# Routed layers of a six-stage Trainium2 kernel: rooms for experts' results, order of the tail, second chunk's norm and the next stage's accumulating loads

## The reference, cut to what matters

```
x = x + 0.5 * routed(norm(x))      # stage routed0
x = x + attention0(norm(x))        # stage attention0, one head, causal, rank 32
x = x + 0.5 * routed(norm(x))      # stage routed1, same weights
x = x + 0.5 * gated(norm(x))       # stage gated0, inner width 704
x = x + attention1(norm(x))        # 16 heads of 128, causal, rotary
x = x + 0.5 * gated(norm(x))       # stage gated1
norm(x)   = (x - mean) / sqrt(var + eps)
routed(x) = sum over each row's 4 chosen of 16 experts (at most 128 rows each):
              w * (silu(x Wg) * (x Wu)) Wd          # inner width 176
            + (silu(x Sg) * (x Su)) Sd              # shared, inner width 352
```

## Time and profile before

| | us |
|---|---|
| median of 3 runs (lowest, highest) | 2019.42 (2014.98, 2020.13) |
| the profiled execution, its own time | 2020.47 |
| its span in the profile | 2018.7 |
| PE busy | 1938.0 (96%) |
| DVE, ACT, POOL busy | 1435.0, 1316.5, 936.9 |

### The profile page before, as it was taken

The page is one execution under the profiler, slowest core; times in us unless marked ns, Lnnn a source line. Parts: engine busy times, 40 slices in busy tenths (PEclk is TensorE's granted clock), DMA queues, the critical chain, the costliest instruction groups (busy, mean ns, idle before and its releaser), DMA issues.

```text
span 2018.7 us, 40238 instructions
## 1 busy us (share of the span) xinstructions
PE 1938.0 (96%) x13726; PEld 1763.0 (87%) x13726; DVE 1435.0 (71%) x3587; ACT 1316.5 (65%) x3367; POOL 936.9 (46%) x961
## 2 busy tenths in 40 slices
PE   7988989898999999999999999999999999999999
PEld 5768867787899999999999999999999999998888
DVE  8368763755878777787877778787777878777753
ACT  4336633444778777777877777787777778776752
POOL 2641126444454536555453645545364554536242
PEclk9999989999999999999999999999999999999999
DMA  7750068500000000000000000000000000000000
GB/s 267 219 100 1 33 195 209 144 1 9 9 9 6 10 6 4 7 9 9 6 9 7 4 7 9 9 7 9 7 4 7 9 9 7 9 6 1 22 27 32
DMA packets 58600, 73.44 MB, mean 36 GB/s; under 512 B 9760, under 2 KB 45216, under 8 KB 58272
## 3 DMA queue, kind: packets, MB, share of 16 engines
q1 hardware_dynamic: 48032, 58.03, 8.9%
q0 software_dynamic: 10368, 12.85, 3.8%
HBM read 51.06 MB, written 19.80 MB: 35 GB/s over the span
## 4 chain that ended last, share of the span: by engine, by line
PE 61%; DVE 12%; ACT 9%; issue 7%; POOL 7%; DMA 4%; SPq 0%; ACTq 0%; POOLq 0%; DVEq 0%
PE phase_scores L1242 16%; PE phase_ring L1300 9%; PE phase_y L167 5%; PE phase_y L166 5%; PE phase_y L165 5%; PE phase_ring L165 4%; PE phase_ring L167 4%; PE phase_ring L166 4%; ACT phase_p L1274 3%; DMA y_rows<-phase_out,phase_rows 3%; DVE phase_scores L1253 2%; POOL phase_rot L2474 1%; POOL phase_straight L2472 1%; PE phase_up_ps L165 1%; PE phase_up_ps L167 1%
## 5 line engine op out<-in xcount | busy, mean ns | idle before, releaser
L1274 ACT ACTIVATE phase_p<-phase_scores,phase_bias 128x512 f32<-128x512 f32 (+3 forms) x680 | 417.5, 628 | 117.3 <-DVE phase_bias L1262 116.7
L1320 DVE TENSOR_TENSOR phase_pt_lo<-phase_ring,phase_pt_hi 128x512 fp32r<-128x512 f32 (+3 forms) x680 | 390.7, 604 | 90.1 <-ACT phase_pt_hi L1315 86.2
L1315 ACT ACTIVATE phase_pt_hi<-phase_ring 128x512 fp32r<-128x512 f32 (+3 forms) x680 | 343.1, 536 | 105.1 <-PE phase_ring L1300 100.8
L1300 PE MATMUL phase_ring<-sb_ident,phase_p 128*128 128x128 f32 x2312 | 340.7, 274 | 12.1 <-ACT phase_p L1274 6.7
L165 PE MATMUL phase_y<-phase_pt_hi,phase_v_hi 128*128 128x256 f32 (+1 forms) x1152 | 341.3, 296 | 6.5 <-DVE phase_y_lo L2448 6.3
L167 PE MATMUL phase_y<-phase_pt_hi,phase_v_lo 128*128 128x256 f32 (+1 forms) x1152 | 321.3, 279 | 0.0
L166 PE MATMUL phase_y<-phase_pt_lo,phase_v_hi 128*128 128x256 f32 (+1 forms) x1152 | 321.2, 279 | 0.0
L1300 PEld LDWEIGHTS phase_ring<-sb_ident,phase_p 128*128 128x128 f32 x2312 | 271.8, 140 | 53.3 <-ACT phase_p L1274 16.9
L1255 DVE TENSOR_REDUCE phase_peaks<-phase_scores 128x1 f32<-128x512 f32 (+1 forms) x408 | 265.8, 666 | 45.8 <-PE phase_scores L1242 43.5
L2472 POOL TENSOR_TENSOR phase_straight<-phase_rot,late_rope 64x512 f32<-64x512 f32 x128 | 163.7, 1279 | 275.5 <-ACT phase_rot L2341 275.4
L2489 POOL TENSOR_TENSOR sb_x<-sb_x,phase_part 128x512 f32<-128x512 f32 x128 | 164.8, 1288 | 253.4 <-ACT phase_part L2376 247.0
(11 more groups left out here) (282 smaller groups left out, 4848.8 us busy)
## 6 DMA issues: line engine op xcount, KB each, us to landing
phase_e_up<-expert_up SPq DMA_DIRECT2D x32, 352.0 KB, 4.7
phase_e_dn<-expert_down SPq DMA_DIRECT2D x32, 256.0 KB, 5.0
y_rows<-phase_zero SPq DMA_DIRECT2D x16, 512.0 KB, 7.8
xn_rows<-phase_ln_xn SPq DMA_DIRECT2D x8, 512.0 KB, 2.9
sb_x<-y_rows POOLq DMA_DIRECT2D x8, 512.0 KB, 6.6
late_raw_qk<-qk SPq DMA_DIRECT2D x16, 256.0 KB, 2.7
sb_x<-x SPq DMA_DIRECT2D x4, 512.0 KB, 5.6
phase_e_up<-y_rows SPq DMA_DIRECT2D x4, 512.0 KB, 4.5
```

What stands on the lines that cost most here:

```text
L1274: act.activation(self.p[:, at:at + width], self.scores[:, at:at + width], ACT.Exp, bias=self.bias[:, t % 2:t % 2 + 1], accum_out=self.sums ...
L1300: done = pe.transpose(bank[:, j * P:(j + 1) * P], self.p[:, (4 * place + j) * P:(4 * place + j + 1) * P], self.core.ident[:])
L1315: act.activation(hi, value, ACT.Copy).then_inc(*self.t_hi.one)
L1320: dve.tensor_tensor(lo, value, as_f32(hi), ALU.subtract).then_inc(*self.t_lo.one)
```

## The change

- `AMONG, BEHIND` go from 6, 12 to 4, 14. Worked out from `plan_order`: among the experts now stand up 6 (behind place 5), gate 7 and round 6 (behind place 10), up 7 and gate 8 (at the last two); up 8 and the two sums of chunk 1 move behind place 15.
- Six rooms for experts' results; DVE waits for `placed[n - 6]`.
- The tail's order and SP's fetch order become (0, array 0), (0, array 1), (1, array 0), (1, array 1); grow (1, 0) comes before scale 0, grow (1, 1) between the last sums. The second chunk is only measured in the tail; attention0 scales and flips it behind its first values, gated0 behind pieces (0, 1) and (0, 2).
- POOL in attention0 and gated0 first waits for `first.normed_v` of chunk 1. Attention0's weights ahead wait for places 10 and 11; its first values' copy waits for grow (1, 1).
- routed1's head: PE does up 0 before the logits, gate 1 before the last transposes of logits, gate 2 before rank; ACT scales and flips chunk 3 ahead of the logits' copies. gated0's norms of chunks 2 and 3 move one to three pieces later.

```diff
-    AMONG, BEHIND = 6, 12
+    AMONG, BEHIND = 4, 14
...
+        more_out = self.raw_dn[:, 0:2, :] if start else sb("out_more", [P, 2, H])[:]
+        self.out_rooms = [self.out[:, n, :] for n in range(4)] + [more_out[:, n, :] for n in range(2)]
...
-        self.first_banks = [[banks[:, b, :] for b in pair] for pair in ((6, 7), (1, 3))]
+        self.first_banks = [banks[:, b, :] for b in (6, 7)]
...
-        order += [("gate", 0), ("up", 0), ("gate", 1), ("up", 1), ("rank",), ("weights",), ("slot",),
-                  ("mark_low",), ("mark",), ("gate", 2), ("round", 0), ("round", 1), ("up", 2),
+        ranked = [("rank",), ("gate", 2)] if self.start else [("gate", 2), ("rank",)]
+        order += [("gate", 0), ("up", 0), ("gate", 1), ("up", 1), *ranked, ("weights",), ("slot",),
+                  ("mark_low",), ("mark",), ("round", 0), ("round", 1), ("up", 2),
...
-        among = {("sums", 1, 1): [("ahead", 0)], ("round", last - 3): [("ahead", 1), ("ahead", 2)], ("up", last - 2): [("ahead", 3), ("grow", 0, 0)],
-                 ("round", last - 2): [("grow", 1, 0)], ("up", last - 1): [("grow", 0, 1), ("measure", 0)], ("up", last): [("grow", 1, 1)],
-                 ("round", last): [("scale", 0)], ("sums", NCH - 2, 1): [("measure", 1), ("flip", 0, 0), ("flip", 0, 1)],
-                 ("sums", NCH - 1, 0): [("scale", 1)], ("sums", NCH - 1, 1): [("flip", 1, 0), ("flip", 1, 1)]}
+        among = {("up", last - 3): [("ahead", 0)], ("sums", 1, 1): [("ahead", 1)], ("round", last - 3): [("ahead", 2)], ("up", last - 2): [("ahead", 3)],
+                 ("round", last - 2): [("grow", 0, 0)], ("up", last - 1): [("grow", 0, 1), ("measure", 0)], ("round", last): [("grow", 1, 0), ("scale", 0)],
+                 ("sums", NCH - 2, 1): [("flip", 0, 0), ("flip", 0, 1)], ("sums", NCH - 1, 0): [("grow", 1, 1)], ("sums", NCH - 1, 1): [("measure", 1)]}
...
-        for b in range(2):
+        for c, b in ((0, 0), (0, 1), (1, 0), (1, 1)):
             sp.wait_ge(*self.placed[b][tag, NE - 2 + b])
...
         if not self.start:
             self.pe_gate(pe, 0)
+            self.pe_multiplier(pe, 0)
...
         self.pe_logits(pe, 3)
+        if not self.start:
+            pe.wait_ge(*self.logits_out[tag, 2])
+            self.pe_gate(pe, 1)
         self.pe_logits_back(pe, (2, 3))
...
+            self.norm.act_rows(act, 3)
             self.act_logits(act, 0)
-            self.norm.act_rows(act, 3)
             self.act_logits(act, 1)
+            self.act_flip(act, 3)
             self.act_logits(act, 2)
-            self.act_flip(act, 3)
...
-                if n >= 4:
-                    dve.wait_ge(*self.placed[n % 2][tag, n - 4])
+                if n >= 6:
+                    dve.wait_ge(*self.placed[n % 2][tag, n - 6])
...
             if nc < NCH and t % 4 == 0:
-                order += [("rows", nc)] * (nc > 1) + [("bias", nc)]
+                order += [("rows", nc), ("bias", nc)]
...
-                order += project(nc)[:2] if nc > 1 else []
+                order += project(nc)[:2]
...
             name = self.names[n]
+            for b in range(2):
+                act.wait_ge(*self.prior.placed[b][self.prior.tag, NE - 6 + b])
...
     def pool(self, pool):
+        pool.wait_ge(*self.first.normed_v[self.tag, 1])
...
                 act.wait_ge(*self.valued[g])
+                if g == 0:
+                    act.wait_ge(*self.prior.grown[self.prior.tag, 1, 1])
...
-    GROWN_NORM = {(1, 0): [("scale", 0, 2)], (1, 1): [("turn", 0, 2)], (1, 3): [("scale", 0, 3)], (1, 4): [("turn", 0, 3)]}
-    GROWN_LATE = {(0, 4): [("measure", 0, 2), ("invert", 0, 2)], (1, 0): [("measure", 0, 3), ("invert", 0, 3)]}
+    GROWN_NORM = {(0, 1): [("scale", 2, 1)], (0, 2): [("turn", 2, 1)], (1, 2): [("scale", 0, 2)], (1, 3): [("turn", 0, 2)],
+                  (1, 4): [("scale", 0, 3)], (1, 5): [("turn", 0, 3)]}
+    GROWN_LATE = {(1, 0): [("measure", 0, 2), ("invert", 0, 2)], (1, 1): [("measure", 0, 3), ("invert", 0, 3)]}
...
         if self.add_y:
+            pool.wait_ge(*self.first.normed_v[tag, 1])
             self.prior.pool_grow(pool, 0)
```

More of the change, by code:

```diff
@@ L688, in pe @@
         for what, *key in self.order:
-            if what == "gate" and (self.start or key != [0]):
+            if what == "gate" and (self.start or key not in ([0], [1])):
                 self.pe_gate(pe, *key)
-            elif what == "up":
+            elif what == "up" and (self.start or key != [0]):
                 self.pe_multiplier(pe, *key)
@@ L1466, in dve_ahead @@
             name = self.names[n]
+            for b in range(2):
+                dve.wait_ge(*self.prior.placed[b][self.prior.tag, NE - 6 + b])
             dve.wait_ge(*self.weight_hi[name])
```

42 lines of the change are left out of this document (20 added, 22 removed).

## The result

| | before | after |
|---|---|---|
| median, us (lowest, highest), 10 runs each on the same chip | 2018.09 (2011.01, 2020.13) | 2026.24 (2020.91, 2028.68) |
| the profiled execution, own time; its span | 2020.47; 2018.7 | 2028.1; 2026.3 |
| ratio after / before, 95% interval | | 1.0040, 1.0029 to 1.0051 |

The changed kernel is 8.1 us slower; the two profiled spans differ by 7.6. The page of the changed kernel: span, busy time, and the shares of the chain that ended last.

A forecast was written before the change was run, and what follows sets the result against it. PE, busy 96% of the span and 61% of the last-ending chain, was taken as the bound. Terms -0.2 + 1.2 - 4.0 + 0.3 + 0.4 = -2.3 from the 2019.42 median gave 2017.1 us; range 2013.4 to 2020.4, wider 2009 to 2024.

The forecast's parts named there:

- Gated0, +0.4: Tail of routed1 and gated0: 2.9 us won at gated0's start and lost in POOL's queue, net +0.4.
- Norms of chunks 2 and 3 one to three pieces later have a chunk of PE work ahead of their need: 0.: Gated0: the later norms of chunks 2 and 3 are covered by PE work and cost 0.
- Attention0, +1.2: Attention0: late by 0.4 us at full clock, 2.1 at half, waiting for POOL's third load; middle taken, +1.2.
- the chain of 4.4 to 5.2 us with nothing beside it: Attention0: chunk 1's inverse, rows, transposes, copy and lo run in order on three engines; next peak at 146.5 to 149.0.
- a sign of being wrong: Attention0: the prediction is wrong if POOL's queue is not what DVE's measure of chunk 2 waits for.
- My four summands there: Attention0, POOL's loads and bias additions before the third load starts: 0.9 + 2.9 + 0.8 + 2.7, given as 7.4 us.
- Rival A: Slower: POOL's hold decides, at attention0's measure of chunk 2 and gated0's h_lo; +3.4 to 2022.8, or 2024.8; chance 0.16.
- its side conditions: Down weights landing at 383.8, half clock in attention0's wait for chunk 1, gated0's pieces waiting for h_lo beyond PE's lead.
- Head, -4.0: Head of routed1: reordering removes PE's gaps and half clock; slot starts at 273.8 instead of 277.75, -4.0 us.
- rival C: Head of routed1: half clock returns at the 2.2 us gap, find waits for PE; -2.0 instead of -4.0, 2019.1; chance 0.14.
- Rooms and spread, +0.1: Both expert loops: rooms give 0 on the path; landings change routed0 by -0.2 and routed1 by +0.3.
- Tail, +0.8: Tail of routed0: round 11 waits some 0.8 us for ACT's copy, so scale 0 starts 0.8 later.

The follow-up runs named there:

- e6: Changed kernel with the routed0-to-attention0 seam as before (tail, fetches, second chunk in the tail, POOL not held); ratio 1.0025 to the kernel before.
- e7: Changed kernel with both seams as before, leaving six rooms, AMONG and BEHIND, and routed1's head; ratio 0.9981 to the kernel before.
- e11: e6 with POOL not held in gated0 and gated0's norms of chunks 2 and 3 where they were before; ratio 1.0004 to the kernel before.
- e1: Changed kernel with POOL no longer held in gated0, attention0's hold kept; ratio 1.0043 to the kernel before.
- e3: e1 with gated0's norms of chunks 2 and 3 behind the pieces they hung behind before; ratio 1.0032 to the kernel before.
- e12: e1 once more, beside the changed kernel on the same chip; ratio 1.0036 to the kernel before.
- e13: e3 once more, beside the changed kernel on the same chip; ratio 1.0020 to the kernel before.
- e5: Changed kernel with the whole routed1-to-gated0 seam as before, routed0's tail and attention0 still changed; ratio 1.0002 to the kernel before.
- e8: e7 with POOL's first bias addition in attention0 held until the second chunk is scaled, loads not held; ratio 0.9963 to the kernel before.
- e14: e7 with the change's two holds of POOL, in attention0 and gated0, loads included; ratio 0.9952 to the kernel before.
- e10: Kernel before with six rooms and AMONG and BEHIND of 4 and 14, nothing else; ratio 0.9993 to the kernel before.
- e4: Kernel before with only the change's edits of routed1's head; ratio 0.9999 to the kernel before.
- c2: The changed kernel itself, timed again in the fourth set; ratio 1.0035 to the kernel before.
- c1: The changed kernel itself, timed again in the second set; ratio 1.0039 to the kernel before.

## Why the prediction was wrong

- **Gated0, +0.4 with bounds of -2.5 and +4: the step that failed.** It measured +8.9 (e6 against e7, tail and late norms included). Its first half held: the down weights came in time (their first use on ACT is at 379.02, I had put them at 380), and h_lo at 388.0, third load at 390, piece (0, 4) at 390.1 were forecast; 388.03, 389.84 and 390.30 came. Then "DVE's pieces follow these, PE's follow DVE's" had the next piece at 393.2, and it came at 396.00, at half clock: DVE's weight rest took 3.92 beside POOL's subtractions and chunk 1's lo stood in front. I counted POOL's queue and gave DVE's no length, nor PE's waits a clock; of the 9.9 us by which G grew, 4.0 are slower matmuls. The second chunk between the pieces, with the new order of the tail, is 4.6 us (e11 against e7).
- **"Norms of chunks 2 and 3 one to three pieces later have a chunk of PE work ahead of their need: 0."** It cost 2.2 and 3.2 us (e1 to e3, e12 to e13). The need was not the next chunk's product but the transposes in PE's own order: chunk 3's hang behind piece (1, 5), which is half as wide, so PE had 1.4 us less work ahead of ACT's scaling; it idled 1.95 instead of 0.56, with half clock behind it in some of the profiles (1.5 us more to the next mark).
- **Attention0, +1.2.** Measured +4.2 (e5 against e7). The stall went, and the chain of 4.4 to 5.2 us with nothing beside it came as written (chunk 1's lo at 146.80, peak at 148.00, forecast 146.5 to 149.0). Too small was its sequel: twelve matmuls of state and action at half clock, 0.43 apart instead of 0.23, are 2.3 us; with them 152.26 moved by +3.5, my bound was +1.9. What I held for the limit was none: chunk 2's measure at 160.18 (L240) was not waiting for POOL's load, which I had named beforehand as a sign of being wrong. (My four summands there make 7.3, not 7.4; the third load began 6.5 behind POOL's release.) That the second chunk's chain and its half clock are the whole of the 4.2 us is read from one profile; no run takes them apart.
- **Rival A** had the sign, but less of the size (+3.4 to +5.4 us, measured +8.1), and the wrong mechanism: gated0's hold costs nothing that can be told from none (some 2 us at most), attention0's was not waited for, and with the second chunk left in the tail attention0's hold gains 4 to 6 us (e7 to e8, where only the addition is held, 3.6; e7 to e14 5.9). Of its side conditions, half clock in attention0's wait and pieces that wait for h_lo did occur; down weights at 383.8 did not. That it came nearest in time is luck.
- **Head, -4.0**: right in its place (-3.9) and in its mechanism (PEclk 0.94 instead of 0.84). Of that, 2.4 reached the end beside rooms and spread (e10 to e7), 0.2 alone (e4). My rival C named the half clock at the find; it came in e4 and in one of three profiles of the changed kernel (c2, 3.09 for the find after 2.62 us of idling), and costs 1.6 us where it comes. The gap alone does not say when: e6 idled 2.62 there too and kept the full clock (1.92).
- **Rooms and spread, +0.1**: -1.4, not told from 0. PE no longer idles for expert 9 in routed1 (it was 2.2), and as forecast that brings nothing. Of the landings, routed0's last came 2.2 earlier in this profile where I gave 0.2 (0.7 in c1's), and 0.8 of it went into the longer fetch.
- **Tail, +0.8**: from the last place's landing to chunk 0's transposes 13.9 instead of 12.3; 0.8 is round 11's wait, as forecast, and the rest the longer fetch.

Three steps of the sum were right (head, tail, the end of the stall). The others fail in one way: I priced each moved piece of work by the engine that the change touched, and left out what stood in order on the other two, and the clock that PE loses while it waits.

## What to carry to other kernels

A norm's chain (DVE, ACT, PE, ACT, DVE) that stood in a seam where PE idled anyway was cheap there; taken out of the seam it needed its own cover on all three engines, each of which works in order, and it had none. Before a wait on a helper engine is blamed, run the kernel without it beside the one with it on the same chip: in gated0 the chain of waits named the hold, and taking it away gained nothing that could be told; in attention0 the hold was worth some 4 to 6 us, but only with the second chunk back in the tail. Read a stretch's length as idle time and slower matmuls apart. And a short operation of DVE with two inputs in SBUF that stands beside a long one of POOL is worth separating: here a wait on the long one did it.
